# Query projections by halves, and an earlier search for the feeding loop's step, in a four-layer hybrid kernel

## The chip, the cores and the metric

The kernel runs on one core of one Trainium2 chip. The metric is the device time of one execution in microseconds, the median of several runs. The profile is of one execution.

## The reference

The input is x of shape (16, 32, 16, 16). Four layers follow each other, each added to its input: a spatial self-attention with 2x2 pooling; a Mamba-like state-space block over 256 positions with 16 states; windowed attention (8 heads, window of 32) and a mixture of eight small experts with the two best of each token; attention within blocks of 32 tokens, whose mask and bias come from a list of 1,048,576 edges, and at last a "feeding" scan, which is what most of the change is about:

```
def step(h, p):                       # scanned over NB = 33 blocks of weights
    op = argmax(h[0, 0, :19])         # one of NOPS = 19 operations, found from the data
    y = attention(h, p['wq'][op], ...)@ p['wo'][op]
    h = where(p['am'][op], y, h)      # only where attn_mask[block, op]
    z = relu(h @ p['w1'][op] + p['b1'][op]) @ p['w2'][op] + p['b2'][op]
    h = where(p['fm'][op], z, h)      # only where ffn_mask[block, op]
```

h is (16, 256, 32) normed tokens. A block whose two masks are both off for the chosen operation changes nothing.

## The kernel before

Channels and batches lie on the 128 partitions (4 groups of 32 channels), and 4 x 256 pixels in the free dimension: NT = 1024 columns, HALF = 512, of which one fills a bank of PSUM. `bank(k, n)` is n banks from k. Every engine has its own program, written out in order, and they meet at semaphores: `eng.wait_ge(sem, value)`. `link(...)` is an instruction followed by its own engine's wait for its end. Inside the loops, `hold(eng, sem, value)` is a wait against a value computed from the step's number i, and an increment of a counter.

**Query projections** (L1171 and L2189). Each of 8 heads has a 128x128 matrix; its product with all 1024 columns (both halves of `xpad`) goes to two banks, and ScalarE copies it to `qm`. Four heads are projected ahead of the first unit, the other four in units 0 and 1. A unit u of eight is four heads of one j of four (hg = u // 4, j = u % 4): scores (`unit_scores`), values, VectorE's merge of two windows, the maximum and shift, ScalarE's exponential, VectorE's sums, GpSimd's weights (L948), VectorE's transposes, GpSimd's bands (L959, L961), and the output matmuls three units behind into banks 6 and 7, which `clear_outputs` clears in unit 2. GpSimd also issues one or two gathers per unit (L867).

**Edge masks before the scan** (L1477 to L1493). VectorE builds one-hot rows in three chunks (`hot_rows`, `weigh_planes`); in the third, the products for delta (`dt_act`, `dtu`) come between the two. GpSimd's first state input (L882) waits for `dtu`.

**Block attention and residual** (L1781 to L1801). VectorE's order is written out: keys, scores, sums, transposes (`block_turned`), then, for both halves, X += projection + bias. TensorE then runs `stream_norm(6, 5, 7)`: both halves centred, a filler matmul, both variances, six filler matmuls.

**Finding the step.** A step is a number, its code: 4 x (steps left) + 2 x (ffn mask) + (attention mask), 0 where both masks are off. There are 33 x 19 = 627, on one partition. `find_step` takes the index of the largest of the first 19 values of the first token, multiplies all 627 codes by its one-hot row, takes the largest (the earliest block), and writes it to `ctrl`. `drop_blocks` then zeroes the codes of the blocks that are past. Each engine loads `ctrl` in a register (`reg_load`).

**The feeding loop.** On SyncE, ScalarE, VectorE and TensorE, two nested loops of six, each with a test whether the code is zero, so that what is left is skipped. A body has two branches: attention (unrolled over 16 batches) and FFN. With these inputs two steps run, both with the FFN alone. In it SyncE loads w1, b1, w2, b2; TensorE runs four filler matmuls and w1 (L2458), ScalarE and VectorE each do bias and relu for two of the four groups, TensorE w2 (L2468); VectorE makes `h_col`, the first 32 columns of the first group, transposes it and finds the next step, while ScalarE writes the whole of `h4` (L1270). Then VectorE drops blocks and adds X + h4 into `x_out`. After the loop a small memset (L1908) releases SyncE's store.

Of the kernel before, what the change touches and what calls it, by code (L numbers as in the profile page):

```python
# [6 lines left out]
ALU = mybir.AluOpType  # L7
# [26 lines left out]
def hybrid_kernel(nc, a, out):  # L34
    with ExitStack() as ctx:
# [265 lines left out]
        ROUNDS = 6  # L301
        assert ROUNDS * ROUNDS >= NB
# [22 lines left out]
        picked = per_op(steps_f[:, 0:STEPS])  # L325
# [108 lines left out]
        FILLED = dict(nat=2, warm=3, bd=4, w2=5, w3=6, mask=7, alone=8, experts=9)  # L434
# [149 lines left out]
        QM_BANK = (0, 2, 4, 6) + (6,) * 4  # L584
# [26 lines left out]
        FFN_PE = G + 1  # L611
        FFN_ACT = 3
        FIND, AFTER = 5, 3
        LINKS = 2 + FIND + AFTER
        FFN_DVE = 2

# [36 lines left out]
        def _(sp):  # L653
# [58 lines left out]
            with sp.Fori(0, ROUNDS) as outer:  # L712
                with sp.If_ne(active, 0):
                    with sp.Fori(0, ROUNDS) as inner:
                        i = outer * ROUNDS + inner
                        with sp.If_ne(active, 0):
                            code, attends, feeds = step_flags(sp, active)
                            at = (STEPS - (code >> 2)).with_bounds(min_val=0, max_val=STEPS - 1)
                            with nc.allow_non_contiguous_dma("small biases"):
                                with sp.If(attends > 0):  # L720
                                    for dst, src in load_attention_step(at):
                                        sp.dma_start(dst, src).then_inc(dma_fa, 16)
                                with sp.Else():
                                    sp.sem_inc(dma_fa, N_STEP)
                                with sp.If(feeds > 0):
                                    dst, src = step_weight(w1_4, "ffn_w1", at)
                                    sp.dma_start(dst, src).then_inc(dma_f, 16)
                                    sp.dma_start(b1_4, step_vector("ffn_b1", at, 1)).then_inc(dma_b1, 16)
                                    dst, src = step_weight(w2_4, "ffn_w2", at, 1)
                                    sp.dma_start(dst, src).then_inc(dma_g, 16)  # L730
                                    hold(sp, ffn_act, FFN_ACT * i + 1)
                                    sp.dma_start(b2_4, step_vector("ffn_b2", at, G)).then_inc(dma_g, 16)
# [1779 lines left out]
```

## Time and profile before

| | us |
|---|---|
| median of 3 runs (624.32 to 626.54) | 625.59 |
| the profiled execution | 628.51 |
| its span | 626.9 |
| TensorE busy | 418.2 (67%) |
| VectorE busy | 478.1 (76%) |
| ScalarE busy | 204.1 (33%) |
| GpSimd busy | 350.9 (56%) |

Mean granted TensorE clock 0.829 of full speed. Of the chain that ended last, 31% is VectorE's, 30% GpSimd's, 19% TensorE's and 12% "issue". In the rows, PE is TensorE's matmul, PEld its weight load, DVE is VectorE, ACT is ScalarE, POOL is GpSimd, SP is SyncE; a trailing q is an engine's sequencer. A timeline row gives start, duration, engine, line, operation, output<-input, shapes, count, and in brackets the idle time before it and what ended it. Rows of one line that follow each other are merged, and the duration is then from the first's start to the last's end.

### The profile page before, as it was taken

What the parts mean: (1) busy time and instruction counts of PE and PEld (TensorE: products, weight loads), DVE (VectorE), ACT (ScalarE), POOL (GpSimd) and SP (SyncE); (2) the same over time, 40 slices, a digit from 0 to 9 for tenths busy, and PEclk for the clock granted to TensorE, in tenths of its full rate; (3) what the DMA queues carried; (4) which work ended last, traced back from release to release, by engine and by line L of the source; (5) the groups of instructions that cost most, each with busy time, mean ns of one, the idle gap of its engine ahead of it and who ended that gap; (6) DMA issues with size and microseconds to landing.
All of it is one profiled execution on the core that took longest, in us unless ns stands there. A gap on an engine that the chain in (4) does not pass through costs nothing.

```text
span 626.9 us, 8773 instructions
## 1 busy us (share of the span) xinstructions
PE 418.2 (67%) x3280; PEld 209.7 (33%) x3290; DVE 478.1 (76%) x622; ACT 204.1 (33%) x227; POOL 350.9 (56%) x307
## 2 busy tenths in 40 slices
PE   6678864676676667667767879687163997554660
PEld 2453323222222223222223335575132435441220
DVE  1998998799999999999996317999416556996332
ACT  2564883223233232323230544221010126112220
POOL 6667004579999999998996321789980000430000
PEclk8986887769999999999999998655566996578775
DMA  8540023935554574555430000000000000000000
GB/s 282 171 136 9 2 85 96 209 82 155 152 149 137 148 181 134 142 161 155 149 105 1 8 6 1 2 2 1 2 22 1 2 0 1 2 3 8 3 5 33
DMA packets 29523, 46.11 MB, mean 74 GB/s; under 512 B 18146, under 2 KB 19588, under 8 KB 28452
## 3 DMA queue, kind: packets, MB, share of 16 engines
q1 hardware_dynamic: 27044, 45.12, 26.0%
q0 software_dynamic: 2368, 0.37, 0.5%
q8 instruction: 29, 0.48, 0.3%
q14 instruction: 18, 0.15, 0.1%
q10 hardware_dynamic: 64, 0.00, 0.0%
HBM read 43.57 MB, written 1.11 MB: 71 GB/s over the span
## 4 chain that ended last, share of the span: by engine, by line
DVE 31%; POOL 30%; PE 19%; issue 12%; ACT 3%; DMA 2%; DVEq 1%; SPq 0%; ACTq 0%; POOLq 0%
POOL dBu L882 14%; POOL hit L867 7%; PE ps L1983 3%; POOL work L959 3%; POOL work L961 3%; DVE hC L1525 2%; PE ps L2193 2%; PE ps L2305 2%; POOL work L948 2%; DVE hst L1504 2%; DVE hC L1295 2%; DVE hC L1291 1%; DVE work L1751 1%; PE ps L2458 1%; PE ps L2220 1%
## 5 line engine op out<-in xcount | busy, mean ns | idle before, releaser
L2121 PE MATMUL ps<-hC,ident 128*128 128x512 f32 x256 | 123.1, 603 | 0.0
L1143 ACT ACTIVATE ps<-work,a_neg 128x1020 f32<-128x1020 f32 x64 | 71.2, 1115 | 155.7 <-DVE hst L1504 102.7
L1504 DVE TENSOR_TENSOR_SCAN hst<-ps,dBu 128x1024 f32<-128x1024 f32 x43 | 98.3, 2287 | 5.1 <-POOL dBu L882 3.8
L2105 PE MATMUL ps<-late,pick_state 96*128 96x512 bf16 x128 | 40.4, 399 | 69.2 <-DVE hC L1525 67.9
L867 POOL DMA_INDIRECT hit<-in_L_attn_edge_values,tab_i x64 | 67.0, 1047 | 29.6 <-DMA hit<-in_L_attn_edge_values,tab_i 20.4
L882 POOL TENSOR_TENSOR dBu<-work,dA 128x1024 f32<-128x1024 f32 x32 | 75.3, 2360 | 7.1 <-DMA dA<-b_rows_all 4.3
L2121 PEld LDWEIGHTS ps<-hC,ident 128*128 128x128 f32 x256 | 49.8, 195 | 43.8 <-issue 35.4
L882 POOL TENSOR_TENSOR dBu<-work,b_sb 128x1024 f32<-128x1024 f32 x16 | 39.8, 2488 | 38.8 <-DVE work L1488 37.3
L1525 DVE TENSOR_TENSOR hC<-hst,ps 128x1024 f32<-128x1024 f32 x43 | 51.5, 1198 | 1.8 <-PE ps L2105 1.1
L1504 DVE TENSOR_TENSOR_SCAN work<-ps,dBu 128x1024 f32<-128x1024 f32 x21 | 48.0, 2287 | 2.0 <-POOL dBu L882 1.3
L2105 PEld LDWEIGHTS ps<-late,pick_state 96*128 96x128 bf16 x128 | 7.9, 99 | 120.9 <-DVE hC L1525 116.9
L996 POOL TENSOR_TENSOR work<-work 128x1024 f32<-128x1024 f32 x3 | 5.7, 1913 | 75.0 <-DVE work L1760 75.0
L882 POOL TENSOR_TENSOR dBu<-work 128x1024 f32<-128x1024 f32 x16 | 37.7, 2359 | 8.3 <-DVE hst L1504 7.9
L1918 PE MATMUL ps<-idle_bf,zero_bf 128*128 128x512 bf16 x90 | 24.8, 421 | 16.6 <-issue 14.2
L1055 ACT ACTIVATE sq<-ps 128x512 f32<-128x512 f32 x12 | 7.2, 597 | 74.1 <-PE ps L1983 56.8
L2220 PE MATMUL ps<-work 32*128 32x64 f32 x512 | 27.4, 344 | 1.1 <-ACT work L1174 1.1
L2244 PE MATMUL ps<-work 128*32 128x64 f32 (+1 forms) x512 | 15.8, 305 | 18.1 <-POOL work L961 17.5
L948 POOL TENSOR_TENSOR work<-work,sm 128x1024 f32<-128x1024 f32 x8 | 15.3, 1918 | 21.5 <-DVE sm L1620 21.4
L2220 PEld LDWEIGHTS ps<-work 32*128 32x128 f32 x512 | 25.7, 256 | 2.3 <-ACT work L1174 1.9
L1525 DVE TENSOR_TENSOR hC<-work,ps 128x1024 f32<-128x1024 f32 x21 | 25.1, 1196 | 0.0
L2232 PE MATMUL ps<-work,w_vu 32*128 32x256 f32 x64 | 16.4, 602 | 12.5 <-DVE work L1634 12.4
L1605 DVE COPY_PREDICATED work<-band,ps 128x1024 f32<-128x1024 int32 x8 | 10.4, 1302 | 16.8 <-ACT work L1182 16.8
(369 smaller groups left out, 833.4 us busy)
## 6 DMA issues: line engine op xcount, KB each, us to landing
dA<-b_rows_all SPq DMA_DIRECT2D x64, 256.0 KB
b_sb<-b_rows_all SPq DMA_DIRECT2D x32, 256.0 KB
work<-b_rows_all SPq DMA_DIRECT2D x32, 256.0 KB
work<-in_L_attn_edge_index SPq DMA_DIRECT2D x6, 1024.0 KB, 7.2
dA<-in_L_attn_edge_index SPq DMA_DIRECT2D x1, 1024.0 KB, 5.3
dBu<-in_L_attn_edge_index SPq DMA_DIRECT2D x1, 1024.0 KB, 8.4
hit<-in_L_attn_edge_values,tab_i POOLq DMA_INDIRECT x64
late<-work SPq DMA_DIRECT2D x12, 64.0 KB, 2.0
```

The source lines that it names most:

```text
L867: nc.gpsimd.indirect_dma_start(out=hit[:, i // C, 0, i % C:i % C + 1], out_offset=None, in_=a["L3_attn_edge_values"].rearrange("(e o) -> e ...
L882: nc.gpsimd.tensor_tensor(dBu[:, i % 2, :], dtu[:, j * NT:(j + 1) * NT], b_buf[i % 4], ALU.mult).then_inc(dbu_done, 1)
L948: nc.gpsimd.tensor_tensor(pairs(s2_buf[u % 3]), pairs(s2_buf[u % 3]), sm2[:, u % 2, :].unsqueeze(2).to_broadcast([P, SEGS, C]), ALU.mult). ...
L959: nc.gpsimd.tensor_tensor(dst[:, :, :, 0, :], src, upto.unsqueeze(1).unsqueeze(1).to_broadcast([P, G, WT, C]), ALU.mult)
L961: nc.gpsimd.tensor_tensor(dst[:, :, 0:WT - 1, 1, :], src[:, :, 1:, :], after.unsqueeze(1).unsqueeze(1).to_broadcast([P, G, WT - 1, C]), AL ...
L1143: nc.scalar.activation(dst[:, :, 1:], src[:, :, 1:], ACT.Exp, scale=a_neg[:, n:n + 1]).then_inc(dA_sb, 1)
L1504: V.tensor_tensor_scan(h_buf[i % 3], dA_ps[k], dBu[:, k, :], 0.0, ALU.mult, ALU.add).then_inc(scan_done, 1)
L1525: V.tensor_tensor(hC[:, k, :], h_buf[i % 3], bank(2, 2), ALU.mult).then_inc(hc_done, 1)
L1918: T.matmul(bank(k), zero_bf[:, :], idle_bf[:, :], start=True, stop=True, skip_group_check=True)
L2105: last = T.matmul(bank(2 + h), pick_state[:, n, :, :].rearrange("p v i -> p (v i)"), parts[:, j * NT + h * HALF:j * NT + (h + 1) * HALF], ...
L2121: last = T.matmul(bank(6 + h), ident[:, :], hC[:, i % 2, h * HALF:(h + 1) * HALF], start=False, stop=(n == S - 1))
L2220: last = T.matmul(bank(g)[:, 2 * C * m:2 * C * m + 2 * C], qm[r, j * WT + m, 4 * hg:4 * hg + 4, :].rearrange("p h q -> p (h q)"), xpad[r, ...
```

## The change

1. The projections go by halves: four heads on half 0 first (banks 4 to 7), then six pairs of heads on one half, two pairs in each of units 0 to 2, in banks 6 and 7. The outputs are cleared in unit 3.
2. In the third chunk of edge masks the delta products come first; GpSimd's first state input also waits for the masks' rows.
3. The codes are made after the block keys, and the best code of each operation is kept (`top_codes`, 19 values) by a reduction over blocks, again in `drop_blocks`. `find_step` works on 19 values.
4. The first half of the block residual is added, normed and searched before the second; `drop_blocks` comes before the second half's norm. TensorE loses its filler matmuls of that norm, and waits for `normed` only in the loop's body.
5. In a step, `h_col` waits for w2's first matmul, no longer for the last; `x_out` is added before `drop_blocks`; b1's load waits for the earlier step's `h4`.
6. Loops of 2, 3, 3 and 2 in place of 6 and 6.

```
-        ROUNDS = 6
+        LEVELS = (2, 3, 3, 2)
...
-        QM_BANK = (0, 2, 4, 6) + (6,) * 4
+        QM_PAIRS = ((0, 1), (2, 1), (4, 0), (6, 0), (4, 1), (6, 1))
...
+        def every_step(nest, eng, active):
+            i = 0
+            for count in LEVELS:
+                i = i * count + nest.enter_context(eng.Fori(0, count))
+                nest.enter_context(eng.If_ne(active, 0))
+            return i
...
                                 sp.dma_start(dst, src).then_inc(dma_f, 16)          # w1
+                        hold(sp, ffn_act, FFN_ACT * i + 1)
                                 sp.dma_start(b1_4, ...).then_inc(dma_b1, 16)
                                 sp.dma_start(dst, src).then_inc(dma_g, 16)          # w2
-                                    hold(sp, ffn_act, FFN_ACT * i + 1)
                                 sp.dma_start(b2_4, ...).then_inc(dma_g, 16)
...
+                    pool.wait_ge(rows_sb, SLOTS // CHUNK)        # state_input(0)
...
+            def first_queries(h):                                # ScalarE
+                act.wait_ge(qm_ps, h + 1)
+                nc.scalar.activation(qm[:, 0:2 * WT, h, :], bank(4 + h)..., ACT.Copy).then_inc(qm_sb, 1)
+            def query_pair(k):
+                h, i = QM_PAIRS[k]
+                act.wait_ge(qm_ps, 4 + k + 1)
+                nc.scalar.activation(qm[:, 2 * WT * i:2 * WT * (i + 1), h:h + 2, :]..., bank(6, 2)..., ACT.Copy).then_inc(qm_sb, 1)
...
+            block_out(0)                                         # ScalarE
+            block_out(1)
+            norm_square(6, 0)
+            block_out(2)
+            norm_root(6, 0, eps5)
+            block_out(3)
+            norm_square(6, 1)
+            norm_root(6, 1, eps5)
...
-                    hot_rows(q % 2, q)                           # VectorE, third chunk
                     dve.wait_ge(dt_log, 1)
                     V.tensor_tensor(dt_act...) ; V.tensor_tensor(dtu...) ; V.memset(dA_ps...)
+                    hot_rows(q % 2, q).then_inc(rows_sb, 1)
                     weigh_planes(V, q % 2, q).then_inc(rows_sb, 1)
...
+            def step_codes():
+                dve.wait_ge(dma_m, 32)
+                dve.wait_ge(filled, FILLED["codes"])
+                ...                                              # the four operations on 627 codes, as before
+                link(V.tensor_reduce(top_codes, codes.rearrange("p b o -> p o b"), AX_X, ALU.max))
...
-                link(V.tensor_tensor(picked, codes_left, one_hot..., ALU.mult))
-                link(V.max(code8[:, :], picked.rearrange("p b o -> p (b o)")))
+                link(V.tensor_tensor(one_hot[:, :], top_codes, one_hot[:, :], ALU.mult))
+                link(V.max(code8[:, :], one_hot[:, :]))
...
             def drop_blocks(link):
                 link(V.tensor_scalar(later...))
                 link(V.tensor_tensor(codes_left, codes, later..., ALU.mult))
+                link(V.tensor_reduce(top_codes, codes_left.rearrange("p b o -> p o b"), AX_X, ALU.max))
...
             last_weights()
+            block_residual(0)
             block_turned(2)
             block_turned(3)
-            ...                                                  # both residuals, then the codes
             link(norm_half(6, 0, h4))
             link(V.transpose(h_t, h4[0:C, 0:C]))
             find_step(link).then_inc(ctrl_ready, 1)
+            block_residual(1)
+            drop_blocks(link)
             norm_half(6, 1, h4).then_inc(normed, 1)
-            drop_blocks(link)
...
                         find_step(slink).then_inc(ctrl_ready, 1) # VectorE, in the loop
-                            drop_blocks(slink)
                         hold(dve, ffn_act, FFN_ACT * i + FFN_ACT + 1)
                         slink(V.tensor_tensor(x_out, X[:, :], h4, ALU.add))
+                drop_blocks(slink)
...
+            block_output(0)                                      # TensorE
+            block_output(1)
+            block_result(0)
+            last_centred(0)
+            block_output(2)
+            last_variance(0)
+            block_output(3)
+            block_result(1)
+            last_centred(1)
+            last_variance(1)
-            stream_norm(6, 5, 7)
-            pe.wait_ge(normed, 2 * 4 + 1)
...
                         keep_warm(4, 7)
+                    pe.wait_ge(normed, 2 * 4 + 1)
...
                         for h in range(2):                       # w2
                             last = T.matmul(bank(h)[C * g:C * g + C, :], w2_4, hid..., start=True, stop=True)
+                            if g == 0 and h == 0:
+                                last.then_inc(ffn_pe, 1)
```

## Rows read from the trace of the kernel before

**Rows 1.** The timeline of all engines, 356 to 374 us.
```profile
359.66 0.69 DVE L1599 TENSOR_TENSOR work<-ps,rstd 128x512 f32<-128x512 f32 x1 [3.88 <-ACT rstd L1050]
...
361.58 7.13 PE L2193 MATMUL ps<-work,w_km 128*128 128x512 f32 x16 [1.25 <-DVE work L1599]
...
368.75 1.02 ACT L1174 ACTIVATE work<-ps 128x1024 f32<-128x1024 f32 x1 [0.69 <-PE ps L2193]
...
369.82 2.01 PE L2220 MATMUL ps<-work 32*128 32x64 f32 x64 [1.11 <-ACT work L1174]
```

**Rows 2.** The timeline, the window weights of unit 1 on GpSimd.
```profile
394.72 1.91 POOL L948 TENSOR_TENSOR work<-work,sm 128x1024 f32<-128x1024 f32 x1 [4.33 <-DVE sm L1620]
```

**Rows 3.** Busy time by stretch: PE, PEld, DVE, ACT, POOL, granted clock, DMA, GB/s.
```profile
392.00:461.00 69.00, 40.77 (x787) 33.48 (x780) 51.13 (x60) 11.47 (x11) 62.01 (x34) 0.52 0.01 2
488.00:507.00 19.00, 18.03 (x49) 7.71 (x48) 9.68 (x8) 0.77 (x1) 0.00 (x0) 1.00 0.00 1
```

**Rows 4.** The timeline from the last block weights to the end.
```profile
559.94 2.37 DVE L1769 STREAM_TRANSPOSE work<-work 128x1024 f32<-128x1024 f32 x2
...
566.31 0.75 DVE L1800 SCALAR_TENSOR_TENSOR X<-ps,b_p,X 128x512 f32<-128x512 f32 x1 [3.37 <-PE ps L1983]
...
570.82 0.69 DVE L1362 TENSOR_TENSOR work<-ps,rstd 128x512 f32<-128x512 f32 x1
571.31 0.63 ACT L1050 ACTIVATE rstd<-rstd 128x512 f32<-128x512 f32 x1
...
574.12 0.14 DVE L1821 CAST ctrl<-code 1x1 int32<-1x1 f32 x1
574.19 0.67 DVE L1362 TENSOR_TENSOR work<-ps,rstd 128x512 f32<-128x512 f32 x1
...
580.68 1.49 PE L1918 MATMUL ps<-idle_bf,zero_bf 128*128 128x512 bf16 x3 [9.21 <-issue]
...
582.10 3.82 PE L2458 MATMUL ps<-work 32*128 32x512 f32 x16
...
586.14 2.48 DVE L1886 TENSOR_SCALAR work<-ps,work 128x1024 f32<-128x1024 f32 x2 [9.04 <-PE ps L2458]
...
591.00 0.24 DVE L1890 TENSOR_SCALAR work<-ps,work 32x32 f32<-32x32 f32 x1 [2.37 <-PE ps L2468]
...
614.42 1.23 DVE L1904 TENSOR_TENSOR work<-X,work 128x1024 f32<-128x1024 f32 x1 [0.34 <-DVE late L1826]
623.42 0.09 DVE L1908 MEMSET later<- 1x33 f32 x1 [7.77 <-issue]
```

**Rows 5.** The timeline, GpSimd's first state input.
```profile
101.08 4.37 POOL L882 TENSOR_TENSOR dBu<-work,b_sb 128x1024 f32<-128x1024 f32 x1 [37.28 <-DVE work L1488]
```

**Rows 6.** The timeline of VectorE, last block keys and first block scores.
```profile
519.73 0.23 DVE L1735 TENSOR_SCALAR work<-work,b_k 128x16 f32<-128x16 f32 x1
525.25 1.26 DVE L1747 TENSOR_TENSOR work<-ps,work 128x1056 f32<-128x1056 f32 x1 [5.28 <-PE ps L2343]
```

**Rows 7.** Groups by line, 574 to 627 us: busy, mean ns, idle before.
```profile
L1818 DVE TENSOR_TENSOR late<-late,one_hot 1x627 f32<-1x627 f32 x2 | 1.6, 799 | 0.3
...
L1816 DVE TENSOR_TENSOR one_hot<-ops_at,best_i 1x19 f32<-1x19 uint32 x2 | 0.3, 166 | 0.3
```

**Rows 8.** TensorE's sequencer at the attention branch: ns min/median/max, first and last start.
```profile
L2410 PEldq COMPARE_BRANCH x2: 220/1814/3408, 576.3 to 596.4; - x2
```

**Rows 9.** Pieces of the chain that ended last: start, us, what.
```profile
574.88 0.04 SPq L712
...
575.24 0.03 SPq L716
...
576.34 2.84 DMA work<-in_L_ffn_ffn_w
...
616.44 0.26 issue
```

More of the change, by code:

```diff
@@ L433, in hybrid_kernel @@
         filled = sem("filled")
-        FILLED = dict(nat=2, warm=3, bd=4, w2=5, w3=6, mask=7, alone=8, experts=9)
+        FILLED = dict(nat=2, warm=3, bd=4, w2=5, w3=6, mask=7, alone=8, experts=9, codes=10)
         consts = sem("consts")
@@ L711, in _ @@
             sp.reg_load(active, ctrl[0:1, 0:1])
[L712 to L730, printed above, removed]
-                                    hold(sp, ffn_act, FFN_ACT * i + 1)
-                                    sp.dma_start(b2_4, step_vector("ffn_b2", at, G)).then_inc(dma_g, 16)
-                                with sp.Else():
-                                    sp.sem_inc(dma_f, 16)
-                                    sp.sem_inc(dma_b1, 16)
-                                    sp.sem_inc(dma_g, 32)
-                            hold(sp, ctrl_ready, i + 2)
-                            sp.reg_load(active, ctrl[0:1, 0:1])
@@ new lines, in _ @@
+            with ExitStack() as nest:
+                i = every_step(nest, sp, active)
+                code, attends, feeds = step_flags(sp, active)
+                at = (STEPS - (code >> 2)).with_bounds(min_val=0, max_val=STEPS - 1)
+                with nc.allow_non_contiguous_dma("small biases"):
+                    with sp.If(attends > 0):
+                        for dst, src in load_attention_step(at):
+                            sp.dma_start(dst, src).then_inc(dma_fa, 16)
+                    with sp.Else():
+                        sp.sem_inc(dma_fa, N_STEP)
+                    with sp.If(feeds > 0):
+                        dst, src = step_weight(w1_4, "ffn_w1", at)
+                        sp.dma_start(dst, src).then_inc(dma_f, 16)
+                        hold(sp, ffn_act, FFN_ACT * i + 1)
+                        sp.dma_start(b1_4, step_vector("ffn_b1", at, 1)).then_inc(dma_b1, 16)
+                        dst, src = step_weight(w2_4, "ffn_w2", at, 1)
+                        sp.dma_start(dst, src).then_inc(dma_g, 16)
+                        sp.dma_start(b2_4, step_vector("ffn_b2", at, G)).then_inc(dma_g, 16)
+                    with sp.Else():
+                        sp.sem_inc(dma_f, 16)
+                        sp.sem_inc(dma_b1, 16)
+                        sp.sem_inc(dma_g, 32)
+                hold(sp, ctrl_ready, i + 2)
+                sp.reg_load(active, ctrl[0:1, 0:1])
@@ L1224, in _, with block_out @@
                 nc.scalar.activation(s3[j], s3[j], ACT.Exp).then_inc(s3_exp, 1)
-            for j in range(J):
+            def block_out(j):
                 act.wait_ge(o3_ps, j + 1)
```

468 lines of the change are left out of this document (233 added, 235 removed).

## The prediction
> **What bounds the kernel now.** I read the page first (execution 628.51 us, span 626.9, so 1.6 us lie around it; the median of the runs is 625.59), then the chain of waits, then the timeline of the stages that the change touches.
>
> The window attention (359 to 461 us) starts with a bare hand-over: the first half of the normed input is ready at 359.66 + 0.69 = 360.35, the projections of four heads start only at 361.58, take 7.13 us for 16 instructions (0.446 each), the last ScalarE copy follows, and the scores start at 369.82 [rows 1]. Nobody else has work there. From 394.72 on the chain is GpSimd's: it idles 4.33 us before that row, for VectorE, and is then busy 62.01 of the 69 us to 461 [rows 2, 3]. So what starts GpSimd earlier moves the whole stage.
>
> The tail is one chain over all engines. VectorE finishes the last transposes, adds the residual, and 4.5 us after that add begins, the first normed half [rows 4]. It finds the step (from 570.82 to 574.26), and the step's first large matmul starts at 582.10. Two steps run. After the second, the last add into x_out ends at 615.65, and the instruction that frees the store is at 623.42, with 7.8 us of pure issue before it.
>
> **The query projections.** Now: eight instructions instead of 16 before the scores, released by the first half alone. Start 360.35 + 0.07 = 360.42; 8 x 0.446 = 3.57, to 363.99; last copy half as long as the 1.02 us of [rows 1] and at most as long (0.51 to 1.02; I take 0.6, near the half because the form is half as wide); scores at 364.7 instead of 369.82: -5.1 us. The copies (0.6) keep up with 0.89 us of matmul per head. The rest of the projections is the 16 instructions of four heads and the eight of the second half, in six pairs over three units instead of four heads over two. The scores of unit 2 need the first two pairs, copied in unit 0 as before. In unit 2 TensorE and ScalarE get a pair more each (2.0 and 1.0 us twice); there is no output matmul in that unit, and ScalarE is busy 11.47 of 69 us in this stretch [rows 3]. GpSimd's row at 394.72 hangs on VectorE's sums of unit 1, before any of the added pairs. So I carry -5.1; the bound from the other side is 0, if the added copies delay the exponentials by what was won.
>
> **Before the scan.** The third chunk's row masks move behind the delta products. GpSimd's first product starts on the end of the masks either way, at 101.1, and takes 4.37 us beside VectorE's last plane product, where others take 2.36 [rows 5]. The masks and the two products change places on one engine, and the scan waits for GpSimd. 0 us; from below -2.0 (a product that costs 2.36), from above +0.6 (a wait more on the same queue).
>
> **Step codes and the first search.** The codes (1254-element cast, three 627-element operations, one reduction added, a copy gone) go in front of the block scores. VectorE is idle 5.28 us there, from 519.96 to 525.25 [rows 6]. Five operations of 0.8 us (one row of four alike that I read: 799 ns for 627 elements [rows 7]) and their links are 4.15 us: hidden, with 1.1 to spare. The new reduction reads with a stride; between 0.72 (the 0.80 of the 627-element search, or less) and 1.6 us I take 0.8, since it is one pass over the same elements. Even 1.6 fits.
>
> Then the first half goes through on its own. VectorE adds it at 559.94 in place of the transposes [rows 4] (its matmul is long ready). Centre, square, mean, logarithm and exponential took 571.94 - 566.31 = 5.63 us from the second add to the end of its root [rows 4]; one half's chain is that at most, also with the output matmul of block 2 between. Normed half at 565.6. The search from there took 3.44 us to 574.26; the multiplication and the search over 627 elements (0.80 + 0.80) become operations on 19 elements (0.17 each), -1.26: step known at 567.8 (-6.5). The second half is added right after, at 567.8, instead of 566.31, which costs 1.5, but its norm no longer stands behind the search: 567.8 + 5.1 + 0.7 = 573.6 against 574.19 + 0.67 = 574.86. So the values are 1.3 us earlier.
>
> What is late next is TensorE's entry into the loop. It waited for 574.86 and started its filler matmuls at 580.68, first weights 0.4 before: 5.4 us of sequencer. In them one compare-and-branch, over the attention body, takes 3408 ns the first time and 220 ns the second [rows 8]. Weights (requested at 576.34, landed 2.84 later [rows 9]) were ready sooner. The new order lets TensorE's queue walk in after its last variance matmul is issued (about 570.8, as the square of half 1 ends at 570.4): -4.05. Two more loop levels cost what SyncE's two cost: 574.88 to 575.28, 0.4 us [rows 9]; I take 0.45 (bounds 0 and 0.9). First FFN matmul at 578.5: **-3.6 us**. Everything else is ready by then (values 573.6, weights 573.3, b1 behind ScalarE's root at 572.9 plus 2.3).
>
> The Trainium skill ("Runtime: NRT & Kernel Launch", Instruction fetch mechanics) says that a taken branch whose target is outside the two resident blocks forces a fetch before execution goes on. By that rule, the trace agrees at 3.4 us for a first jump; it would also let a shifted or deeper loop miss again, which the third and fifth rivals below price by rows.
>
> **Each step.** h_col waits no longer for TensorE's end but for its first matmul; then VectorE's own last bias-and-relu binds. It ends at 588.62, h_col starts at 591.00 [rows 4]; with 0.33 of waits it starts at 588.95: -2.05. The shorter search: -1.26. Together **-3.3 us** per step, twice; the next weights' request, their 3 us and the FFN behind them follow it. TensorE's 12 filler matmuls end before those weights come.
>
> **The end.** The step's found flag is now 3.6 + 3.3 + 3.3 = 10.2 earlier (602.8 for 612.98), but the full result only 602 + 1.1 = 603.1 (ScalarE's pass over h4, 1.11). x_out: 603.2 to 604.4. drop_blocks, which used to lie before x_out, comes after it, and has the reduction: 0.22 + 0.80 + 0.80 with three gaps of 0.15 and the last hold: the flag is loaded at 607.1 instead of 615.97: -8.9. That is 1.3 given back of 10.2, and 2.1 if the reduction costs 1.6. Leaving the loop: from 616.38 to 623.42, 7.04 us, the queue skips four inner and five outer iterations. A branch comes every 0.38 (the first piece of issue starts at 616.44 [rows 9], the next at 616.82), two to a skip, 0.75; the other 7.04 - 6.75 = 0.3 are the two loop ends, 0.15 each. With levels 2, 3, 3, 2, two steps leave 0 + 2 + 2 + 1 = 5 skips: 4 x 0.75 = 3.0, less two more loop ends of 0.15: **-2.7**. Tail: -8.9 - 2.7 = **-11.6**.
>
> Sum: -5.1 + 0 - 11.6 = -16.7; against its own execution 628.51 gives 611.8, and from the median of the runs, 2.9 lower, 625.59 - 16.7 = **608.9**, say 609.0.
>
> **Rivals.**
> 1. *The query gain is absorbed.* The added pairs delay units 1 to 3 and GpSimd starts its train as before. Against it: the row at 394.72 waits for unit 1, where nothing is added. For it: TensorE is the busiest engine but GpSimd and VectorE there, 40.77 of 69 us, at a granted 0.52 [rows 3]. 609.0 + 5.1 = 614.1. Chance 0.10.
> 2. *The first search is early for nothing*: TensorE's queue does not pass its variance matmuls as early as I think, and only the values' 1.3 less 0.45 arrives, 0.85 for 3.6: 611.7. Against: the fillers at 580.68 waited for nothing but the queue. Chance 0.07.
> 3. *One more missed jump on the path.* The loop's code has moved; a jump that was 220 ns in the second step costs 3408 again, +3.2: 612.2. Chance 0.09.
> 4. *The clock falls elsewhere.* The experts' stage (488 to 507) is 18.03 of 19 us TensorE at a granted 1.00, between stretches at half [rows 3]; shifted by 5 us it could start low; a quarter of it at 1.2 GHz is +4.5: 613.5. Chance 0.06.
> 5. *Slower.* Every taken branch of the exit misses, because four levels spread over the block's ends: ten branches by about 3.2 (3408 - 220 ns [rows 8]) are +32, 641. It decides from six misses (16.7 / 3.2 = 5.2). Against: the 18 branches of the present exit take 0.38 each, over the same body. For: nothing but that first jump. Chance 0.03.
>
> **From there to the numbers.** My sum has 0.65. Its own range is 606 to 612: below by the -2.0 before the scan and a level that costs nothing, above by the strided reduction (+0.8), the dearer levels (+0.9 in all) and 1 us in unit 0. Rivals 2, 3 and 4 lie at 611.7 to 613.5, rival 1 at 614.1, so 605.5 to 615.0 leaves little but the fifth and part of the first. Measurements of this kernel can tell 0.3%, 1.9 us, from nothing. Faster 0.95 (all but the fifth and a pile-up of the others), same 0.02, slower 0.03.
>
> **What would show it.** Scores of unit 0 about 9 us after the first VectorE add of that norm, 5 less than now, and GpSimd's second weights row as far earlier; if only the first is seen, rival 1. Codes inside the hole before the first block scores, whose row stays put against the keys. The found flag 8 us after the last weights product, TensorE's fillers at about 577 minus 5.1. h_col 0.3 after VectorE's second relu product. Five skips and 4.4 us before the last small memset. TensorE's or VectorE's branches of over 1 us beyond the first jump would show rivals 3 or 5. The forecast is wrong if the second step's FFN doesn't start 6.9 us earlier than now against the block weights.

## The result, and the profile after

| | before | after |
|---|---|---|
| median of 4 runs each (range) | 625.99 us (624.32 to 626.54) | 618.99 us (617.3 to 619.79) |
| ratio, with its 95% interval | | 0.9889 (0.986 to 0.9918) |
| profiled execution, its span | 628.51, 626.9 us | 619.79, 618.2 us |
| mean granted clock | 0.829 | 0.827 |

The change makes the kernel 7.0 us faster, where 16.7 were forecast; 619 lies above the range. A second measurement of it (a0_again, below) gives 0.9876 (0.9856 to 0.9896). The ratios below leave out a single slow execution, of 1303.63 us, one of the six of e1, whose median is 612.64 us with it and 612.21 without.

The timeline of all engines, 360 to 369 us, and GpSimd's weights row of unit 1, answer to [rows 1, 2]:

```profile
360.46 0.69 DVE L1626 TENSOR_TENSOR work<-ps,rstd 128x512 f32<-128x512 f32 x1 [4.41 <-ACT rstd L1056]
...
361.20 3.70 PE L2223 MATMUL ps<-work,w_km 128*128 128x512 f32 x8
...
364.94 0.60 ACT L1188 ACTIVATE work<-ps 128x512 f32<-128x512 f32 x1 [0.26 <-PE ps L2223]
...
365.68 2.02 PE L2255 MATMUL ps<-work 32*128 32x64 f32 x64 [0.78 <-ACT work L1188]
...
387.95 1.91 POOL L954 TENSOR_TENSOR work<-work,sm 128x1024 f32<-128x1024 f32 x1 [3.84 <-DVE sm L1647]
```

Eight matmuls stand ahead of the scores where 16 did, and ScalarE's copy takes 0.60 us, as estimated. GpSimd's row is 6.77 us earlier. About 2 of those are one slow group of projections in the profiled execution of before (four matmuls at 378.34 take 3.59 us, the other groups of four 1.98): from the end of the second X half of that stage to this row it took 38.94 us there, but 36.67 to 37.15 in three other kernels with the same code, and 31.91 here.

The other end of that train: the row after which the first search can begin, before and after. It is VectorE's last product with the block weights; it ends at 559.90 and 553.07, 6.83 us earlier. Nothing to speak of was won or lost between the weights row and this one.

```profile
558.68 1.22 DVE L1779 TENSOR_TENSOR work<-work 128x1024 f32<-128x1024 f32 x1
```

```profile
551.85 1.22 DVE L1806 TENSOR_TENSOR work<-work 128x1024 f32<-128x1024 f32 x1
```

So the tail, where 11.6 us were expected, gave 9.10 - 6.83 = 2.3 (the last memset is at 614.32 for 623.42). Its timeline, VectorE and TensorE, against [rows 4]:

```profile
553.11 0.75 DVE L1841 SCALAR_TENSOR_TENSOR X<-ps,b_p,X 128x512 f32<-128x512 f32 x1
...
553.91 2.07 PE L2015 MATMUL ps<-X,centerer 128*128 128x512 f32 x2 [3.67 <-DVE X L1841]
...
560.71 0.69 DVE L1389 TENSOR_TENSOR work<-ps,rstd 128x512 f32<-128x512 f32 x1 [4.58 <-ACT rstd L1056]
...
562.75 0.14 DVE L1829 CAST ctrl<-code 1x1 int32<-1x1 f32 x1
562.82 0.73 DVE L1841 SCALAR_TENSOR_TENSOR X<-ps,b_p,X 128x512 f32<-128x512 f32 x1
...
565.42 2.08 PE L2015 MATMUL ps<-sq,averager 128*128 128x512 f32 x2 [0.69 <-ACT sq L1061]
...
568.98 0.69 DVE L1389 TENSOR_TENSOR work<-ps,rstd 128x512 f32<-128x512 f32 x1 [3.12 <-ACT rstd L1056]
...
573.05 1.88 PE L1950 MATMUL ps<-idle_bf,zero_bf 128*128 128x512 bf16 x4 [5.56 <-issue]
...
576.45 3.82 PE L2507 MATMUL ps<-work 32*128 32x512 f32 x16 [1.52 <-DVEq L1912]
...
581.58 4.67 PE L2517 MATMUL ps<-work 128*32 128x512 f32 x16 [1.31 <-ACT work L1292]
...
583.82 0.24 DVE L1922 TENSOR_SCALAR work<-ps,work 32x32 f32<-32x32 f32 x1 [0.87 <-PE ps L2517]
...
587.93 1.22 DVE L1935 TENSOR_TENSOR work<-X,work 128x1024 f32<-128x1024 f32 x1 [1.30 <-ACT work L1297]
590.63 1.29 DVE L1836 TENSOR_REDUCE work<-late 1x19 f32<-1x627 f32 x1
...
594.04 3.82 PE L2507 MATMUL ps<-work 32*128 32x512 f32 x16 [4.19 <-DVEq L1912]
...
614.32 0.09 DVE L1940 MEMSET later<- 1x33 f32 x1 [5.08 <-issue]
```

Here are four things that the forecast doesn't have. Each w1 group (L2507) is held back last not by TensorE's own queue or by weights but by L1912, on VectorE's queue, for 1.52 and 4.19 us. From the start of a half's add (L1841) to the start of its normed product (L1389) there are 7.60 us for the first half and 6.16 for the second, where the forecast had 5.63 and 5.1. Of the four pairs of matmuls over a half (L2015, centring and variance), the first and the last take 2.07 and 2.08 us, the two between 1.29 and 1.13; the w2 group (L2517) takes 4.67 us for the 3.39 that it had. And after x_out VectorE still has `drop_blocks` to do, which ends in a reduction of 1.29 us.

What L1912 is, the source says: the Else side of the attention branch, where VectorE increments `attn_dve`. The chain of waits shows when it comes, for the first step and, in the second fence, for the second (start, us, what):

```profile
572.62 3.42 issue
576.04 0.03 DVEq L1912
...
576.45 1.19 PE ps L2507
```

```profile
590.63 1.30 DVE work L1836
...
592.23 0.32 DVEq L1939
...
593.34 0.24 issue
593.57 0.03 DVEq L1912
...
594.04 1.19 PE ps L2507
```

In the first step VectorE's own jump over the attention body takes 3.42 us; in the second, 0.24, but it comes only after `drop_blocks` (591.93) and the load of the flag (592.23). In both steps VectorE was thus the last to enter, and TensorE, which needs nothing of the attention branch in these steps, waited for it.

The same increment in the trace of the kernel before (ns min/median/max, first and last start):

```profile
L1880 DVEq EVENT_SEMAPHORE  x2: 21/21/21, 581.3 to 599.3; - x2
```

It came at 581.3 and 599.3, and the w1 groups started at 582.10 and 600.53. So this entry was 0.8 and 1.2 us from binding before the change, though no row names it as what w1 waited for.

The tail in parts, from the profiles of the kernels below. W is the end of VectorE's product with the last block weights, F1 and F2 are the starts of the two w1 groups, M the last memset.

| us | W to F1 | F1 to F2 | F2 to M | W to M |
|---|---|---|---|---|
| before | 22.20 | 18.43 | 22.89 | 63.52 |
| after | 23.38 | 17.59 | 20.28 | 61.25 |
| forecast for after | 18.6 | 15.1 | 18.2 | 51.9 |
| e1, wait moved | 21.82 | 14.92 | 20.67 | 57.41 |
| e2, fillers | 20.87 | 16.26 | 20.24 | 57.37 |
| e3, drop first | 23.64 | 16.39 | 19.35 | 59.38 |
| e4, whole norm | 21.43 | 17.54 | 20.25 | 59.22 |
| f1, all three | 19.77 | 14.73 | 18.17 | 52.67 |
| f2, wait, drop, whole norm | 21.15 | 13.65 | 16.67 | 51.47 |
| f3, wait, fillers | 19.80 | 14.43 | 18.97 | 53.20 |
| a0, the changed kernel again | 23.52 | 17.52 | 20.24 | 61.28 |
| b2, the tail of before | 21.23 | 18.05 | 24.23 | 63.51 |
| b4, best code kept | 20.43 | 17.63 | 23.04 | 61.10 |

(Forecast: 22.20 - 3.6; 18.43 - 3.3; and 22.89 less 3.3 and 2.7 plus the 1.3 given back. Each row is one execution. The changed kernel's two agree within 0.14; b2 has the code of before from W on, and its three parts differ from before by 0.4 to 1.3 us, as each also holds the clock that its matmuls ran at.)

### The profile page after: what moved, and what is told of

Same layout as the page of the kernel before. It is cut to its first block, busy times and chain, and to the rows that moved or that the text cites. A ratio compares the mean times of both kernels' runs of the same rounds, so it can differ in the third digit from the quotient of the medians.

```text
span 618.2 us, 8775 instructions
## 1 busy us (share of the span) xinstructions
PE 414.6 (67%) x3283; PEld 206.4 (33%) x3283; DVE 477.4 (77%) x625; ACT 204.3 (33%) x229; POOL 351.2 (57%) x307
## 4 chain that ended last, share of the span: by engine, by line
DVE 31%; POOL 31%; PE 20%; issue 12%; ACT 3%; DMA 2%; DVEq 1%; ACTq 0%; POOLq 0%; SPq 0%
POOL dBu L888 14%; POOL hit L872 7%; PE ps L2015 4%; POOL work L965 3%; POOL work L967 3%; DVE hC L1552 2%; PE ps L2338 2%; POOL work L954 2%; DVE hst L1531 2%; DVE hC L1322 2%; PE ps L2223 2%; DVE hC L1318 1%; PE ps L2507 1%; DVE work L1778 1%; PE ps L2137 1%
## 5 line engine op out<-in xcount | busy, mean ns | idle before, releaser
L2255 PE MATMUL ps<-work 32*128 32x64 f32 x512 | 24.5, 324 | 0.8 <-ACT work L1188 0.8
L2255 PEld LDWEIGHTS ps<-work 32*128 32x128 f32 x512 | 23.4, 238 | 1.6 <-issue 1.6
L2267 PE MATMUL ps<-work,w_vu 32*128 32x256 f32 x64 | 14.6, 541 | 10.5 <-DVE work L1661 10.5
L2279 PEld LDWEIGHTS ps<-work 128*32 128x32 f32 x512 | 13.6, 173 | 21.4 <-POOL work L967 20.2
```

The source lines that it names most:

```text
L2255: last = T.matmul(bank(g)[:, 2 * C * m:2 * C * m + 2 * C], qm[r, j * WT + m, 4 * hg:4 * hg + 4, :].rearrange("p h q -> p (h q)"), xpad[r, ...
L2279: last = T.matmul(bank(6 + j // 2)[C * g:C * g + C, q0:q0 + w * C], vm_buf[u % 4][:, g * N + m * C:g * N + m * C + C], lu_buf[u % 2][:, g, ...
```

## Experiments on the changed kernel

Ratios are to the kernel before on the same chip, with 95% intervals. The theory is that three edits which go with the change, not its purpose, take back what it wins: TensorE's wait for VectorE, the filler matmuls that are gone, and `drop_blocks` behind x_out. The rivals are that the norm by halves is itself the loss, and that the forecast's gains were never there.

**e1_no_dve_wait.** TensorE's wait on `attn_dve` stands at the end of its attention branch, which is not taken in these steps:

```
                     per_batch(0, w4[:, 3, :], y4).then_inc(attn_pe, 1)
+                    hold(pe, attn_dve, ATTN_DVE * i + ATTN_DVE)
                 with pe.Else():
...
                     hold(pe, dma_f, 16 * i + 16)
-                    hold(pe, attn_dve, ATTN_DVE * i + ATTN_DVE)
```

> The changed kernel, with TensorE's wait for attn_dve moved into the attention branch (there, and only there, is h4 VectorE's). Theory W: the FFN of both steps started late because TensorE waits for a count that VectorE gives only when it has entered the loop's body, after x_out and drop_blocks: in the changed kernel's timeline the two w1 groups start 1.52 and 4.19 us after TensorE's last fillers, both released by VectorE's queue. Then step 1's w1 group starts with the fillers' end (about 1.5 us earlier) and step 2's with the weights (landed about 591.7, 1.9 us earlier): 3.4 us less, about 615.6. Theory K (clock alone): the starts move to nothing but the time stays within 1 us of 619.0, since the matmuls run at half speed later anyway.

Measured: 612.64 us, ratio 0.9768 (0.9746 to 0.9791), about 6.8 us less than the changed kernel's 0.9876 and twice the 3.4 that I expected. TensorE's timeline:

```profile
574.41 3.82 PE L2507 MATMUL ps<-work 32*128 32x512 f32 x16
579.57 3.39 PE L2517 MATMUL ps<-work 128*32 128x512 f32 x16 [1.34 <-ACT work L1292]
...
589.33 3.82 PE L2507 MATMUL ps<-work 32*128 32x512 f32 x16 [2.35 <-DMA work<-in_L_ffn_ffn_w]
```

The wait's time is gone in the first step (-1.56 from W) and its place is taken by the weights' DMA in the second (F1 to F2 -2.67), which is what the forecast had bind. With no gap in front of w1 the first step's w2 group takes 3.39 us again; the second step's takes 4.80, for 4.41. From W to M the profiled execution is 3.84 us shorter than the changed kernel's. It took 615.52 us, the longest of the five, 2.9 above the median, so where the other 3 of the 6.8 us are gained no trace shows. With the fillers of e2 in place the same edit is worth 4.7 us by the ratios (f3 against e2) and 4.2 from W to M. So the traces show some 4 us as the wait's.

**e2_fillers.** Filler matmuls as in the other norms: before each centring, before and after the last variance.

```
             block_result(0)
+            keep_warm(6, 3)
             last_centred(0)
...
             block_result(1)
+            keep_warm(2, 5)
             last_centred(1)
+            keep_warm(1, 4)
             last_variance(1)
+            keep_warm(6, 4)
```

> The changed kernel with filler matmuls put back around the two halves of the last norm: six ahead of the first centring, two ahead of the second, one before and six after the second variance. Theory K: without them the granted clock was 0.5 from 559.8 to 580.3 us, and matmuls that took 1.1 us per half took 2.07 and 2.08, w2's groups 4.67 and 4.41 instead of 3.39. With them the halves take 1.1 each, the second half is normed 1 to 2 us earlier and w2 takes 3.4: 3 to 4 us less, about 615.5. Theory W: the halves get faster, but the loop's groups start when VectorE arrives, which moves by the 1 to 2 us only: 617 to 618. If fillers change no matmul's duration, the clock isn't theirs.

Measured: 617.47 us, ratio 0.9845 (0.9816 to 0.9874), some 2 us less than the changed kernel, with intervals that overlap. TensorE:

```profile
565.68 1.13 PE L2015 MATMUL ps<-sq,averager 128*128 128x512 f32 x2 [0.47 <-ACT sq L1061]
...
575.17 4.06 PE L2511 MATMUL ps<-work 32*128 32x512 f32 x16 [1.78 <-DVEq L1912]
580.30 3.39 PE L2521 MATMUL ps<-work 128*32 128x512 f32 x16 [1.07 <-ACT work L1292]
```

The last variance takes 1.13 us for 2.08, the first centring 1.38 for 2.07. From a half's add to its normed product there are 6.00 and 5.23 us for 7.60 and 6.16, and the second normed half is there 14.69 us after W, not 16.60. L1912 is still what w1 waits for. The w2 group takes 3.39 for 4.67, but that can't be put down to these fillers alone: e4 below has that norm's fillers too, and 4.62. Nor was the changed kernel's clock low from 559.8 us on, as my expectation has it: its granted clock is 1.00 to 563.5, and 0.50 from 565.4 to 580.3.

**e3_drop_first.** `drop_blocks` stands ahead of the wait for h4 and x_out, as before the change.

```
                 find_step(slink).then_inc(ctrl_ready, 1)
+                drop_blocks(slink)
                 hold(dve, ffn_act, FFN_ACT * i + FFN_ACT + 1)
                 slink(V.tensor_tensor(x_out, X[:, :], h4, ALU.add))
-                drop_blocks(slink)
```

> The changed kernel with drop_blocks ahead of the x_out add inside the loop, as in the kernel before. Theory W: VectorE has 1.3 us idle there waiting for h4, so the 2.6 us of drop_blocks cover it; it reaches the next body 1.3 us earlier and the last memset 1.0 us earlier: 2.2 us less, 616.8. Rival (the order was right): x_out late by 1.3 us costs as much at the end, 619 to 620.

Measured: 617.39 us, ratio 0.984 (0.9814 to 0.9866), some 2.3 us less than the changed kernel, again with intervals that overlap. F1 to F2 is 1.20 shorter and F2 to M 0.93. VectorE's timeline:

```profile
586.65 0.80 DVE L1834 TENSOR_TENSOR late<-late,later 1x627 f32<-1x627 f32 x1
587.59 1.29 DVE L1836 TENSOR_REDUCE work<-late 1x19 f32<-1x627 f32 x1
589.22 1.23 DVE L1936 TENSOR_TENSOR work<-X,work 128x1024 f32<-128x1024 f32 x1 [0.34 <-DVE work L1836]
```

The two operations fill the time in which VectorE stood idle for ScalarE's h4 (1.30 us at 587.93 above). The change put them behind it, in each step.

**e4_whole_norm.** The block residual and the last norm in the order of before (both halves added, one norm with its fillers), `find_step` and the loops as changed.

```
-            block_residual(0)
             block_turned(2)
             block_turned(3)
+            block_residual(0)
+            block_residual(1)
...
-            block_residual(1)
-            drop_blocks(link)
             norm_half(6, 1, h4).then_inc(normed, 1)
+            drop_blocks(link)
...
-            last_centred(0)
             block_output(2)
-            last_variance(0)
             block_output(3)
             block_result(1)
-            last_centred(1)
-            last_variance(1)
+            stream_norm(6, 5, 7)
```

> The changed kernel with both halves of the block residual and the last norm in the order of the kernel before (both residuals after the transposes, search after the first half's norm, fillers between), everything else as changed. It prices the first-half search alone. Theory H: the half order costs more than it brings, since the first w1 group starts 23.4 us after the last block weights product instead of 22.2: 1 to 3 us less than the changed kernel, about 617. The forecast's view: the early search is worth 2 us or more: 621 or more.

Measured: 619.76 us, ratio 0.9894 (0.9871 to 0.9918): the same as the changed kernel, and a miss for what I expected. In its profile the last w1 wait is the same one (first its last product with the block weights, which ends at W, and the first group of expert matmuls):

```profile
483.57 3.54 PE L2335 MATMUL ps<-work,x 128*128 128x512 f32 x4 [0.97 <-DVE work L1744]
...
553.96 1.23 DVE L1803 TENSOR_TENSOR work<-work 128x1024 f32<-128x1024 f32 x1
...
573.00 1.88 PE L1947 MATMUL ps<-idle_bf,zero_bf 128*128 128x512 bf16 x4 [7.48 <-issue]
576.62 3.82 PE L2501 MATMUL ps<-work 32*128 32x512 f32 x16 [1.75 <-DVEq L1909]
```

By the medians the earlier first search, which was to bring the entry forward, is neither gain nor loss. The trace says more. Counted from W, w1 starts at 21.43 us with the early search undone and at 23.38 with it, and W to M is 2.0 us shorter without it, as theory H has it: by halves the flag comes earlier (9.82 us after W for 11.77), but the second normed half later (16.60 for 12.37), and VectorE, whose entry w1 waits for, has to norm it first. That the whole time is the same all the same is because this execution reaches W 2.1 us later (555.19 for 553.07); 1.6 of these are its first group of expert matmuls, 3.54 us where the changed kernel's takes 1.96. That group lies in code which the edit doesn't touch, and whether the other five executions have it no trace shows. So the early search brings nothing here, and may cost up to 2 us.

**f1_all_three.** The edits of e1, e2 and e3 together.

> The changed kernel with all three repairs: TensorE's attn_dve wait only in the attention branch, fillers back around the last norm, drop_blocks ahead of x_out in the loop. If waits and clock are both causes and independent: first w1 group about 19.9 us after the last block weights product (23.4 changed, 20.9 with fillers alone, 21.8 without the wait alone), second 14.9 later, memset 19.4 later, so 7 us less than the changed kernel's tail of 61.25, ratio 0.977 or below. If one covers the other, no better than the run without the wait alone (0.9768).

Measured: 610.9 us, ratio 0.9752 (0.9722 to 0.9783), the fastest version and 15.5 us under the kernel before. TensorE and VectorE:

```profile
570.98 4.46 PE L2511 MATMUL ps<-work 32*128 32x512 f32 x16
576.13 3.39 PE L2521 MATMUL ps<-work 128*32 128x512 f32 x16 [0.70 <-ACT work L1292]
...
585.71 3.48 PE L2511 MATMUL ps<-work 32*128 32x512 f32 x16 [2.23 <-DMA work<-in_L_ffn_ffn_w]
...
603.88 0.09 DVE L1940 MEMSET later<- 1x33 f32 x1 [5.07 <-issue]
```

W to M is 52.67, where the forecast had 51.9. The three gains don't add up in full (6.8, 2 and 2.3 us less than 0.9876 would be 0.970): with the wait gone, the weights' DMA is what the second step waits for in e1 and in f1.

**f3_wait_fillers** leaves out e3's edit from it, **f2_whole_norm** has e1's and e3's edits with the norm of e4, and **a0_again** is the changed kernel itself, on the same chip.

> The changed kernel with two of the three repairs, the attn_dve wait and the fillers, and drop_blocks after x_out as changed. Additive theory: 1.0 us (end of the last step) to 2.2 us more than with all three (0.9752), 0.977 to 0.979. If the order no longer matters once TensorE doesn't wait for VectorE: only the last step's 1.0, 0.977.

> The kernel with all three repairs, but with the last norm whole, as before the change (both residuals after the transposes, fillers of that norm as in the kernel before). It prices the first-half search once nothing else hides it. Theory E (TensorE's entry into the loop binds, not the search): the entry is 5.4 us behind the last variance matmul in either order, first w1 group 20 to 21 us after the last block weights product for 19.8 with the search by halves: 0 to 1 us slower than that kernel, ratio 0.975 to 0.977. The forecast's view (search early by 6.5, entry early by 3.6): 3 us or more slower, 0.980 or above.

> The changed kernel itself, unchanged, beside the other three, as their reference on this chip. Both theories: ratio within 0.986 to 0.992, and in its trace the w1 groups released by VectorE's queue again.

Measured: f3 611.59 us, 0.977 (0.9749 to 0.9792); f2 612.13 us, 0.9784 (0.976 to 0.9808); a0 618.25 us, 0.9876 (0.9856 to 0.9896). The last of them shows that the result repeats. Next to the other two edits, e3's is worth 0.2% at most, within the intervals. And with the wait repaired the earlier search is worth 0.3%, between what the two theories had, and the intervals don't separate it from nothing: F1 is 1.4 us earlier after W in f1 than in f2, but the steps behind it are 2.6 us longer. In TensorE's timeline of f2 the second step's w1 takes 2.02 us:

```profile
589.94 2.02 PE L2501 MATMUL ps<-work 32*128 32x512 f32 x16 [1.79 <-DMA work<-in_L_ffn_ffn_w]
```

In f1 it takes 3.48. In 8 us around it the granted clock is 1.00 in f2 and 0.83 in f1. Why TensorE has the full clock there in f2 alone is not settled; no run varied the clock of that stretch by itself.

## Experiments on the kernel before: one part of the change each

**b1_levels.** Loops of 2, 3, 3 and 2 alone, on all four engines:

```
-        ROUNDS = 6
+        LEVELS = (2, 3, 3, 2)
...
+        def every_step(nest, eng, active):
+            i = 0
+            for count in LEVELS:
+                i = i * count + nest.enter_context(eng.Fori(0, count))
+                nest.enter_context(eng.If_ne(active, 0))
+            return i
```

> The kernel before with loops of 2, 3, 3 and 2 in place of 6 and 6, and nothing else. The forecast's term: the exit loses 2.7 us (7.77 of idle before the last memset becomes 5.1), the entry gains 0.4 on each queue, so 2.3 us less than before in the profile, ratio about 0.996. Rival (the deeper nest costs at entry, as a new missed jump): TensorE's compare-and-branch over the attention body appears a second time at over 3 us, and the ratio is 1.00 or more.

Measured: 624.97 us, ratio 0.9963 (0.9935 to 0.9991), -2.3. VectorE's exit:

```profile
619.21 0.09 DVE L1907 MEMSET later<- 1x33 f32 x1 [5.08 <-issue]
```

5.08 us for 7.77 [rows 4], the forecast's 2.7 to 0.01. In this one execution the rest of the tail is longer, though: W to F1 by 0.7, F1 to F2 by 0.2, and F2 to M is 1.2 shorter and not 2.7, its second w2 group taking 4.38 us for 3.39. W to M is 63.26. Executions of one tail differ by as much (b2 above), so the exit's row and the medians speak for the 2.3, and the sum of this trace doesn't.

**b2_queries.** The query projections by halves alone:

```
-            pe.wait_ge(normed, 2 * 2)
+            pe.wait_ge(normed, 2 * 2 - 1)
+            for h in range(4):
+                first_queries(h)
```

> The kernel before with the query projections by halves, and nothing else. In the changed kernel GpSimd's second weights row came 31.9 us after that stage's X add instead of 38.9, so 7 us less rather than the forecast's 5.1. Theory Q: the stage alone gives 6 to 7 us, ratio 0.989 to 0.991, and so nearly all of what the change brought. Rival: it gives the forecast's 5.1 (0.992), and the rest was the changed kernel's own luck with the clock in unit 0, where a projection group took 1.98 us for 3.59.

Measured: 620.89 us, ratio 0.9914 (0.9883 to 0.9946), -5.4. GpSimd, for the row of [rows 2]:

```profile
387.78 1.91 POOL L949 TENSOR_TENSOR work<-work,sm 128x1024 f32<-128x1024 f32 x1 [3.83 <-DVE sm L1629]
```

**b3_hcol.** `h_col` after w2's first matmul, and b1's load behind the earlier step's h4:

```
-        FFN_PE = G + 1
+        FFN_PE = G + 2
...
+                                        if g == 0 and h == 0:
+                                            last.then_inc(ffn_pe, 1)
                                 last.then_inc(ffn_pe, 1)
```

> The kernel before with h_col released by w2's first matmul, and b1's load behind the hold that this needs; nothing else. The forecast's term is 2.05 us off each of two steps. Theory W: the flag is found 2 us earlier, but drop_blocks and x_out still end when h4 and VectorE allow: with drop_blocks first, as here, VectorE gets on about 1.5 us earlier per step and the weights 2 earlier, so 3 us less, ratio 0.995. If VectorE's arrival binds wholly, 0.997 or above.

Measured: 620.92 us, ratio 0.9928 (0.99 to 0.9956), -4.5, more than the 3 us expected. VectorE:

```profile
585.28 0.24 DVE L1890 TENSOR_SCALAR work<-ps,work 32x32 f32<-32x32 f32 x1
```

`h_col` starts with no idle time, for 2.37 us in [rows 4]; F1 to F2 is 2.61 shorter and F2 to M 2.04.

**b4_topcodes.** The codes ahead of the block scores and the best code of each operation kept; norm, order and loops as before:

```
+                link(V.tensor_tensor(one_hot[:, :], top_codes, one_hot[:, :], ALU.mult))
+                link(V.max(code8[:, :], one_hot[:, :]))
-                link(V.tensor_tensor(picked, codes_left, one_hot...
-                link(V.max(code8[:, :], picked...
...
+                link(V.tensor_reduce(top_codes, codes_left.rearrange("p b o -> p o b"), AX_X, ALU.max))
```

> The kernel before with the best code kept per operation: codes made ahead of the block scores, the reduction there and in drop_blocks, the search over 19 values; order of the halves, of drop_blocks and x_out as before. The forecast's term: 1.26 us off each of three searches. Since the reduction measured 1.29 us (not 0.8), it is theory R that the two cancel wherever drop_blocks lies on VectorE's way to the next body: found flag 1.26 earlier in each search, step 2's w1 group no earlier than 0.5 us, end of the second step within 0.3: 0.5 to 1.8 us less than before. The forecast's view: the first search and step 1 give it fully, 2.5 us less.

Measured: 626.08 us, ratio 1.0 (0.9974 to 1.0025): nothing, and less than I expected. TensorE's two w1 groups:

```profile
578.07 3.71 PE L2464 MATMUL ps<-work 32*128 32x512 f32 x16 [0.41 <-DVEq L1886]
...
595.70 3.43 PE L2464 MATMUL ps<-work 32*128 32x512 f32 x16 [2.12 <-DVEq L1886]
```

L1886 is again VectorE's increment in the Else branch. In both steps the kernel now reaches the wait that TensorE has on VectorE's entry. In the loop, what is won in finding the step is spent before VectorE comes to its branch: the search is 1.26 us shorter, `drop_blocks` has a reduction of 1.28, and from the start of `h_col` to the end of x_out there are 6.77 us for 6.60. For the first search the trace doesn't say nothing: W to F1 is 0.8 us shorter than in b2, and W to M is 61.10 us for 63.5. But this execution, 623.84 us, is the fastest of twelve, so the forecast's gain is neither shown nor refuted within the 1.6 us of the interval.

The four parts alone sum to -2.3 - 5.4 - 4.5 + 0 = -12.2 us. Together with the earlier search they measure -7.0 to -7.7. Parts need not add up, but the missing 4.5 to 5 us, and 3 more, are what e1 to e3 together bring back (f1: -15.5).

## Why the prediction was wrong

**The step that failed** is TensorE's entry: "First FFN matmul at 578.5: -3.6 us. Everything else is ready by then (values 573.6, weights 573.3, b1 ...)". From W, F1 is +1.2 us and not -3.6 (against b2, +2.2). Two things are wrong in it.

The list left out the one semaphore that comes from no data: `attn_dve`, raised by VectorE on its way past the branch not taken. Before, it was hidden by 0.8 us only (581.3 against w1 at 582.10 [rows 4]). The list asked when each value is ready, and not where each engine's queue is. Behind the second normed half VectorE still has x_out (to 570.94), the flag's load, four levels of loops and the jump of 3.42, and comes to the increment at 576.04: 22.97 us after W, where before it was 21.4. Without this wait F1 is at W + 21.82 (e1): 1.6 of the 4.8 us by which the entry was missed.

The other 3.2 are the norm by halves. The forecast's "one half's chain is that at most" put it at 5.63 us and the second at 5.1, for which it gives no row; they measured 7.60 and 6.16. So the second normed half came 16.60 us after W, where I had 13.7 and before had 14.96: 1.6 later than before, not 1.3 earlier. TensorE's queue comes to its jump 14.8 us after W for 16.4, 1.6 earlier and not 4.05, and the jump takes 4.65 us and not 3.41. With the fillers back the two chains measure 5.74 and 5.24, and F1 is at W + 19.77 (f1), 1.2 above the forecast's 18.6.

**Each step, -3.3**: F1 to F2 -0.8, by the same wait. h_col was right in mechanism, 0.87 us after VectorE's second product rather than 0.3 (0 in f1, where w2's first matmuls run faster); alone it is worth -4.5 us in two steps (b3; -4.1 forecast). The shorter search is -1.26 on VectorE, and in the loop 0 in the end (b4): TensorE is let in by the same VectorE that now does the reduction. That reduction is a term I mis-sized within its bounds: 1.29 us for the 0.8 that I took.

**The end, -8.9.** I charged `drop_blocks` behind x_out once, at the exit, with 1.3 us. It lies on the path of each step, because VectorE's entry gates w1 (e3: -1.20 in F1 to F2, -0.93 at the end). The other 1.0 us of the 2.1 by which F2 to M was missed is the second w2 group, 4.41 us for the 3.39 of before.

**Clock.** I priced the experts' stretch (rival 4) and not the tail, where the change takes the norm's fillers away. The granted clock from 553 to 573 us is 0.67, where before it was 0.80 from 560 to 581, and 0.93 in e2 (0.97 in f1). The low clock comes late in it: 1.00 (2.4 GHz) from 559.8 to 563.5, and 0.50 (1.2 GHz) from 565.4 to 567.6, where the last variance takes 2.08 us for the 1.13 that it takes with fillers. The Trainium skill ("TensorE: Matmul & The Clock Gate", "What's actually happening") says that the array's clock is full or half by how busy it has lately been; the trace agrees in the two levels and in that the fillers raise it, from 0.67 to 0.97. What the clock did to w2 is less clear: the group took 4.50 to 4.67 us wherever w1 had waited for VectorE at the low clock (the changed kernel, e3, e4), with the norm's fillers (e4) or without, and 3.39 in e2, where w1 had waited 1.78 us as well, but the granted clock of the 7 us before it was 0.84 and not 0.50 as in e4. Busy time per stretch (granted clock stands right after the last bracket), the changed kernel and f1:

```profile
553.00:573.00 20.00, 11.04 (x268) 5.30 (x268) 9.86 (x19) 4.58 (x8) 0.00 (x0) 0.67 0.04 8
559.80:563.50 3.70, 1.95 (x97) 1.01 (x86) 2.55 (x11) 1.22 (x3) 0.00 (x0) 1.00 0.00 0
565.40:567.60 2.20, 2.08 (x2) 0.50 (x2) 0.46 (x1) 0.07 (x1) 0.00 (x0) 0.50 0.05 16
```

```profile
551.00:569.00 18.00, 10.72 (x279) 5.16 (x278) 10.07 (x19) 4.59 (x8) 0.00 (x0) 0.97 0.04 9
```

**First search.** The flag came 9.82 us after W for 14.36, -4.5, not -6.5: the first half's chain, 7.60 us for 5.63, is the difference, and with fillers it is gone (7.95 in f3, -6.4).

**Right**: the queries (-5.1; b2 -5.4), nothing before the scan (GpSimd's product of [rows 5] takes 4.16 us at 100.55), the codes hidden ahead of the block scores (from GpSimd's weights row to W 165.12 us, before 165.18), the exit (-2.70), the first missed jump where it was, and no jump missed at the exit. Rivals 1, 3 and 5 didn't occur. Rival 4 didn't in the changed kernel, whose experts' stretch keeps a granted 1.00 (the clock fell in the tail); in the profiled executions of e4 and e2 the first expert group did start low (3.54 and 3.75 us for 1.96), +1.6 to +1.8 us and not +4.5. Rival 2, a first search that is early for nothing, came nearest: TensorE's queue did pass its variance matmuls later than I thought. But the values didn't arrive 1.3 earlier either, and with the semaphore on top the entry lost 4.8 us of its forecast (+1.2 for -3.6) where the rival had 2.75. Repaired in its three places, the kernel is at 610.9 us, where 609 were forecast.

## To carry to other kernels

When a chain is shortened, list for the engine that ends it every semaphore it waits for, those that a branch not taken gives back too, and ask for each where the giving engine's instruction queue stands, not when data is ready. Keep a wait that only one branch needs inside that branch. Work split in halves for the sake of the first half needs a line in the sum for the end of the second, which here came 1.6 us later than before the change. An edit that removes filler matmuls or moves work behind a wait belongs in the sum with its own line, even where the work itself is the same.

## What the runs showed of the hardware

- A first far jump over the attention body costs not TensorE alone: 4646 ns on TensorE (218 the second time), 3.42 us on VectorE (0.24); on TensorE the first jump took between 3.40 us (f1, e4) and 5.09 (e3) over the same kind of body, 3.41 before the change [rows 8], and no run shows what sets it. In the profile of the changed kernel (ns min/median/max):

```profile
L2457 PEldq COMPARE_BRANCH  x2: 218/2432/4646, 567.9 to 588.1; - x2
```

- A reduction of 627 values of one partition to 19 maxima, read with a stride of 19 values, takes 1.29 us, where products over the same 627, and one maximum over all of them, take 0.80. No run separates the stride from the 19 outputs.
- The same group of 16 matmuls takes 3.39 us at the full clock and up to 4.84 (e3, second step) where it starts at the half one. A gap in front of w1 doesn't decide it alone: behind gaps of 1.52 (after) and 1.75 us (e4) w2 takes 4.67 and 4.62, behind 1.78 (e2) and 1.55 (before, second step) 3.39.
